# Post-LN block on 8 cores: draining six instead of four queued layer-norm pieces per output slab

## The chip, the cores and the metric

The kernel runs on all 8 cores of one Trainium2 chip. Each core computes one of 8 batch rows with the same program; nothing is exchanged between cores. The time is the device time of the slowest core, in microseconds.

## The reference

One layer of a recurrent block with post-layer-norm, input x of shape (8, 2048, 1024). Cut to what matters:

```python
xg = gelu(x)
# for fwd and bwd: x1 = xg@Wx+bx; gates = sigmoid(x1@Wg..+b..); h = linear_scan(a, xin); y = h@Wo+bo
x2 = (x_fwd + x_bwd) / 2 + x
attn = gelu(x2) @ ld_W + ld_b + x
x = layernorm(x + attn)                        # LN1
y = clip((x @ sign(weights).T) * scale + bias, -100, 100)
x = layernorm(x + y)                           # LN2
```

## The kernel before

Everything is kept transposed: 1024 features in 8 slabs (index `o`, or `k` when contracted) of 128 partitions, 2048 tokens along the free axis, cut into two halves `h` of 1024 tokens. The stages follow one another: gelu of x, the two input projections, gates and scans forward and backward, the output projections, then the linear layer `Wld` with the first layer norm, then the sign-weight layer with the second.

`Builder` writes one instruction list per engine, in the order in which the Python code calls `bd.op` and `bd.mm_group`. An engine executes its list strictly in that order; semaphores make it wait for what other engines produce. There is no scheduler: where a call stands in the code is where the instruction stands in its engine's list.

The change lies in the linear stage (lines 799 to 878). For each half h and each output slab o:

- TensorE runs one group of 16 matmuls of 128x512 (line 152 emits every matmul), into PSUM buffer `slot = o % 2`; called group 0 to group 7 here. Group o needs that the VectorE operation at L838 of slab o-2 has read the buffer.
- In the second half only, the queue `bg` has pieces in it: `drain_bg(n)` takes up to n of them and emits their instructions at this place, ahead of the slab's own ScalarE and VectorE operations.
- ScalarE doubles the input slab (L833), VectorE adds PSUM, bias and that (L838) and so writes `r1`; this is what frees the PSUM buffer. ScalarE squares `r1` (L845 in the first half, L860 in the second).
- In the second half the statistics of two slabs (8 matmuls by a column of ones, into PSUM slots 2 and 3) follow each of groups 4, 5, 6 and 7, if `len(bg) <= 8`.

`bg` holds the first half's layer norm, 18 pieces in this order: 0 and 1 ScalarE on the sums (L605, L609), 2 VectorE variance (L612), 3 ScalarE Ln (L615), 4 ScalarE Exp (L619), 5 the split of the reciprocal deviation into a high and a low bf16 row (ScalarE L629, then VectorE L632), 6 its broadcast to 128 partitions (TensorE, 2 matmuls of the high and 2 of the low row, then the ScalarE copy L652), 7 VectorE product (L667), 8 the split of the product (L629, L632), 9 its broadcast (4 matmuls, L652), and 10 to 17 the four pairs of VectorE operations of 128x2048 that apply the norm: multiply (L704) and add (L711). The result is read first by the sign-weight stage, after all 8 groups.

Of the kernel before, what the change touches and what calls it, by code (L numbers as in the profile page):

```python
# [171 lines left out]
def build_program():  # L172
# [68 lines left out]
    def ps_ap(slot, lo, hi):  # L241
        return ps_t[slot].ap()[:, ps_off[slot] + lo: ps_off[slot] + hi]

    def vcol(nm, o):
        return vecs_sb[:, VCOL[nm] + o: VCOL[nm] + o + 1]
# [91 lines left out]
    def wtile(arena_ap, o, k):  # L337
        return arena_ap[:, o * 1024 + k * 128: o * 1024 + (k + 1) * 128]
# [154 lines left out]
    def sgn_prep(oc):  # L493
        if wtB[0] is None:
            wtB[0] = Buf("wt0", deps=woslabs[4:6])
            wtB[1] = Buf("wt1", deps=woslabs[6:8])
        sl = oc % 2
        bd.op("sync",
              lambda e, oc=oc, sl=sl:
              e.dma_start(wt_ap[sl], w_hbm["Wffn"].ap()[:, oc * 1024:(oc + 1) * 1024]),  # L500
              writes=[wtB[sl]], inc="dX", step=16)
        bd.op("vector",
              lambda e, oc=oc, sl=sl:
              e.tensor_scalar(A4.ap()[:, 8192 + oc * 1024: 8192 + (oc + 1) * 1024],
                              wt_ap[sl], 0.0, 0.5, ALU.is_ge, ALU.subtract),
              reads=[wtB[sl]], writes=[sgnB], inc="dv")
# [8 lines left out]
    def xc_dma(xcb, o, h, sl):  # L515
        bd.op("sync",
              lambda e, o=o, h=h, sl=sl:
              e.dma_start(xc56_ap[sl], x_hbm.ap()[o * 128:(o + 1) * 128,
                                                  h * HF:(h + 1) * HF]),
              writes=[xcb[sl]], inc="dX", step=16)  # L520
# [69 lines left out]
    def stats_tiles(src_ap_fn, src_buf, k, slot):  # L590
        tiles, treads = [], []
        for t in range(2):
            tiles.append((ones_sb.ap()[:],
                          src_ap_fn(k, t),
                          ps_ap(slot, t * 512, (t + 1) * 512)[0:1, :],
                          k == 0, k == CH - 1))
            treads.append([src_buf, onesB])
        bd.mm_group(tiles, treads, group_reads=(), writes=[PS[slot]])
# [182 lines left out]
    def drain_bg(n):  # L781
        for _ in range(n):
            if bg:
                bg.pop(0)()
# [11 lines left out]
    def emit_sq6_until(j):  # L796
        while sq6_emitted[0] <= j and sq6_pend:
            sq6_pend.pop(0)()
            sq6_emitted[0] += 1

    r1B_h, r1view_h = {}, {}
    for h in range(2):
# [8 lines left out]
        for o in range(CH):  # L811
            if o + 3 < CH:
                xc_dma(xc6, o + 3, h, (o + 3) % 4)
            sl = o % 2
            slot = o % 2
            tiles, treads = [], []
            for k in range(CH):
                for t in range(2):
                    tiles.append((wtile(A4.ap()[:, 0:8192], o, k),
                                  A3.ap()[:, k * 2048 + h * HF + t * 512:  # L820
                                          k * 2048 + h * HF + (t + 1) * 512],
                                  ps_ap(slot, t * 512, (t + 1) * 512),
                                  k == 0, k == CH - 1))
                    treads.append([g2[k * 2 + h], WldS[o]])
            bd.mm_group(tiles, treads, group_reads=(), writes=[PS[slot]])
            if h == 0 and len(pending_stats) > 1:
                pending_stats.pop(0)()
            if h == 0 and sgn_q:
                sgn_prep(sgn_q.pop(0))
            drain_bg(4)  # L830
            xsl = o % 4
            bd.op("scalar",
                  lambda e, sl=sl, xsl=xsl: e.activation(u_ap[sl], xc56_ap[xsl],  # L833
                                                         AF.Copy, scale=2.0),
                  reads=[xc6[xsl]], writes=[uB[sl]], inc="sc")
            bd.op("vector",
                  lambda e, slot=slot, sl=sl, o=o, r1view=r1view:
                  e.scalar_tensor_tensor(r1view[:, o * 1024:(o + 1) * 1024],  # L838
                                         ps_ap(slot, 0, 1024), vcol("ldb", o),
                                         u_ap[sl], ALU.add, ALU.add),  # L840
                  reads=[PS[slot], uB[sl], vecsB], writes=[r1B[o]], inc="dv")
            if h == 0:
                bd.op("scalar",
                      lambda e, o=o, sl=sl, r1view=r1view:
                      e.activation(rsq_ap[sl], r1view[:, o * 1024:(o + 1) * 1024],  # L845
                                   AF.Square),
                      reads=[r1B[o]], writes=[rsqB[sl]], inc="sc")

                def _stats(o=o, sl=sl, r1view=r1view, r1B=r1B):
                    stats_tiles(lambda k, t, r1view=r1view:  # L850
                                r1view[:, k * 1024 + t * 512: k * 1024 + (t + 1) * 512],
                                r1B[o], o, 2)
                    stats_tiles(lambda k, t, sl=sl: rsq_ap[sl][:, t * 512:(t + 1) * 512],
                                rsqB[sl], o, 3)
                pending_stats.append(_stats)
            else:
                sq6_pend.append(lambda o=o, r1view=r1view, r1B=r1B: bd.op(
                    "scalar",
                    lambda e, o=o, r1view=r1view:
                    e.activation(rsq6_ap[o], r1view[:, o * 1024:(o + 1) * 1024],  # L860
                                 AF.Square),
                    reads=[r1B[o]], writes=[rsqS6[o]], inc="sc"))
                if o >= 2:
                    emit_sq6_until(o - 2)

                def _stats(o=o, r1view=r1view, r1B=r1B):
                    emit_sq6_until(o)
                    stats_tiles(lambda k, t, r1view=r1view:
                                r1view[:, k * 1024 + t * 512: k * 1024 + (t + 1) * 512],
                                r1B[o], o, 2)  # L870
                    stats_tiles(lambda k, t: rsq6_ap[k][:, t * 512:(t + 1) * 512],
                                rsqS6[o], o, 3)
                pending_stats.append(_stats)
                if o >= 4 and len(bg) <= 8:
                    while len(pending_stats) > (CH - 1 - o):
                        pending_stats.pop(0)()
# [201 lines left out]
```

How the kernel before makes its waits and increments, by code:

```python
        def thunk(e, wl=tuple(wl), emits=tuple(emits), tok=tok, step=step):  # L118
            for s, v in wl:
                e.wait_ge(sems[s], v)
            inst = None
            for em in emits:
                inst = em(e)
            if tok is not None:
                inst.then_inc(sems[tok[0]], step)
# [18 lines left out]
        def thunk(e, head=tuple(head), per=tuple(per), tiles=tuple(tiles),  # L144
                  tok=tok):
            for s, v in head:
                e.wait_ge(sems[s], v)
            inst = None
            for (lh, rh, oa, st, sp), wl in zip(tiles, per):
                for s, v in wl:
                    e.wait_ge(sems[s], v)
                inst = e.matmul(oa, lh, rh, start=st, stop=sp)
            inst.then_inc(sems[tok[0]], 1)
# [830 lines left out]
    def final_wait(e):  # L984
        for base in ("dO", "dX", "dG"):
            for j in range(Builder.DMA_POOL):
                nm = f"{base}{j}"
                if bd.counts.get(nm, 0):
                    e.wait_ge(bd.sems[nm], bd.counts[nm])
```

## Time and profile before

| what | us |
|---|---|
| median of 2 runs | 746.49 (746.29 to 746.69) |
| the profiled execution's own time | 744.0 |
| span of its slowest core (core 5) | 742.5 |
| spans of all cores | 722.7 to 742.5 |
| TensorE busy in the span | 629.4 |
| VectorE busy | 327.4 |
| ScalarE busy | 349.4 |

The time is the slowest core's; the span runs from that core's first to its last instruction. The shares of busy time are averages over stages that have different limits.

### The profile page before, as it was taken

Reading aid. Unit: us, or ns where it says so; the run is one execution under the profiler, and the core shown is the slowest. Engines: PE = TensorE matmul, PEld = TensorE weight load, DVE = VectorE, ACT = ScalarE, POOL = GpSimd, SP = SyncE. Lnnn points to the kernel's source line nnn. Section 1 sums busy time; section 2 is a strip of 40 time slices with the busy share of each in tenths; the row PEclk is TensorE's granted clock in tenths of the full one; section 3 lists DMA queues with packets and bytes.
Section 4 is the critical chain, followed back from the end, with each engine's and each line's share of the span. In section 5 each row is a group of like instructions: output and inputs, shape, how many; then the busy total and the mean of one; then the engine's idle time right before and its main releaser. Section 6 shows DMA issues by size and latency. Waiting matters only on the chain.

```text
span 742.5 us, 7192 instructions; the slowest of 8 cores (722.7 to 742.5 us)
## 1 busy us (share of the span) xinstructions
PE 629.4 (85%) x2720; PEld 265.2 (36%) x2720; DVE 327.4 (44%) x191; ACT 349.4 (47%) x258; POOL 50.8 (7%) x96
## 2 busy tenths in 40 slices
PE   0349999999999999999999858997998769679660
PEld 0004444444444444444444323443332224224220
DVE  0000000003767767767763120213348638838846
ACT  2442322326687687787771120203375347747710
POOL 2010000000000000000131110100000000000000
PEclk9999999999999999999999998999999888869855
DMA  8997000003222322322439999815753000003205
GB/s 175 249 199 116 1 0 1 1 0 43 43 31 42 43 30 42 43 31 40 72 47 168 203 200 150 178 45 173 212 166 104 1 0 1 1 0 113 115 0 226
DMA packets 23217, 61.33 MB, mean 83 GB/s; under 512 B 2704, under 2 KB 2704, under 8 KB 23184
## 3 DMA queue, kind: packets, MB, share of 16 engines
q0 software_dynamic: 13248, 25.17, 22.9%
q1 hardware_dynamic: 8208, 29.42, 13.2%
q10 hardware_dynamic: 1728, 6.29, 2.8%
q8 instruction: 22, 0.36, 0.2%
q14 instruction: 11, 0.09, 0.0%
HBM read 75.55 MB, written 8.39 MB: 113 GB/s over the span
## 4 chain that ended last, share of the span: by engine, by line
PE 63%; DMA 15%; DVE 11%; issue 5%; ACT 4%; SPq 0%; DVEq 0%; ACTq 0%; POOLq 0%
PE psA L152 32%; PE psB L152 31%; DMA A<-x 6%; DMA A<-Wof 4%; DMA A<-Wob 3%; DVE A L944 2%; DMA A<-Wffn 2%; DVE A L743 2%; DVE A L704 1%; DVE A L757 1%; DVE A L838 1%; ACT srbf L629 1%; DVE srbf L632 1%; DVE A L950 1%; DVE srows L612 1%
## 5 line engine op out<-in xcount | busy, mean ns | idle before, releaser
L152 PE MATMUL psA<-A 128*128 128x512 bf16 x1536 | 359.3, 392 | 60.9 <-ACT A L329 21.5
L152 PEld LDWEIGHTS psA<-A 128*128 128x128 bf16 x1536 | 150.4, 100 | 263.9 <-issue 97.6
L152 PE MATMUL psB<-A 128*128 128x512 bf16 x1024 | 227.8, 381 | 2.0 <-DVE A L568 2.0
L152 PEld LDWEIGHTS psB<-A 128*128 128x128 bf16 x1024 | 100.6, 98 | 124.5 <-issue 5.3
L429 DVE TENSOR_SCALAR A<-A,dvec_sb 128x2048 f32<-128x2048 f32 x16 | 20.6, 1286 | 170.4 <-ACT A L425 170.4
L440 DVE TENSOR_TENSOR A<-A 128x2048 f32<-128x2048 f32 x16 | 36.7, 2292 | 51.0 <-ACT A L433 51.0
L573 ACT ACTIVATE A<-A,dvec_sb 128x1024 bf16<-128x1024 f32 x16 | 18.4, 1148 | 83.1 <-DVE A L568 83.1
L152 PE MATMUL psB<-A,ones_sb 128*1 128x512 bf16 x128 | 37.7, 439 | 13.7 <-DVE A L950 11.2
L425 ACT ACTIVATE A<-psB,vecs_sb 128x2048 f32<-128x2048 f32 x16 | 31.5, 1967 | 32.0 <-PE psB L152 32.0
L431 ACT ACTIVATE A<-A 128x2048 f32<-128x2048 f32 x16 | 30.6, 1910 | 23.8 <-DVE A L429 23.8
L568 DVE SCALAR_TENSOR_TENSOR A<-psA,A 128x1024 f32<-128x1024 f32 x8 | 9.8, 1225 | 72.1 <-PE psA L152 59.1
L438 DVE TENSOR_TENSOR A<-A 128x2048 f32<-128x2048 f32 x16 | 36.6, 2284 | 0.0
L452 DVE TENSOR_TENSOR_SCAN A<-A 128x2048 bf16<-128x2048 f32 x8 | 35.4, 4425 | 0.9 <-DVE A L440 0.2
L446 DVE TENSOR_TENSOR_SCAN A<-A 128x2048 bf16<-128x2048 f32 x8 | 35.4, 4426 | 0.8
L356 ACT ACTIVATE A<-psB,vecs_sb 128x2048 bf16<-128x2048 f32 x8 | 15.7, 1967 | 40.9 <-PE psB L152 40.9
L356 ACT ACTIVATE A<-psA,vecs_sb 128x2048 bf16<-128x2048 f32 x8 | 15.7, 1967 | 35.8 <-PE psA L152 35.8
L421 ACT ACTIVATE A<-psA,vecs_sb 128x2048 f32<-128x2048 f32 x16 | 31.5, 1970 | 0.2
L433 ACT ACTIVATE A<-A 128x2048 f32<-128x2048 f32 x16 | 30.6, 1910 | 0.2
L838 DVE SCALAR_TENSOR_TENSOR A<-psA,vecs_sb,A 128x1024 bf16<-128x1024 f32 x16 | 20.5, 1281 | 20.5 <-ACT A L833 9.6
L329 ACT ACTIVATE A<-A 128x1024 bf16<-128x1024 f32 x16 | 16.0, 1048 | 24.5 <-DMA A<-x 24.5
L152 PEld LDWEIGHTS psB<-A,ones_sb 128*1 128x1 bf16 x128 | 10.3, 91 | 39.9 <-issue 32.5
L933 ACT ACTIVATE A<-psA,dvec_sb 128x1024 f32<-128x1024 f32 x16 | 19.2, 1202 | 10.2 <-PE psA L152 6.4
(59 smaller groups left out, 353.4 us busy)
## 6 DMA issues: line engine op xcount, KB each, us to landing
A<-x SPq DMA_DIRECT2D x40, 512.0 KB, 8.2
A<-x ACTq DMA_DIRECT2D x8, 512.0 KB, 15.2
A<-Wof POOLq DMA_DIRECT2D x16, 256.0 KB, 11.2
A<-Wob POOLq DMA_DIRECT2D x16, 256.0 KB, 13.2
A<-Wffn SPq DMA_DIRECT2D x8, 512.0 KB, 6.1
out<-A SPq DMA_DIRECT2D x8, 512.0 KB, 3.8
A<-Wxf POOLq DMA_DIRECT2D x8, 256.0 KB, 32.4
A<-Wxb POOLq DMA_DIRECT2D x8, 256.0 KB, 22.5
```

What stands on the lines that cost most here:

```text
L152: inst = e.matmul(oa, lh, rh, start=st, stop=sp)
L356: e.activation(xb_arena.ap()[:, o * 2048:(o + 1) * 2048], pst.ap()[:], AF.Identity, bias=vcol(bias_name, o)),
L421: e.activation(gx_ap[p], psA.ap()[:], AF.Sigmoid, bias=vcol(bgx_name, o)),
L425: e.activation(ga_ap[p], psB.ap()[:], AF.Sigmoid, bias=vcol(bga_name, o)),
L429: e.tensor_single_scalar(ab_ap[p], ga_ap[p], ae_col(d, o), ALU.mult),
L431: bd.op("scalar", lambda e, p=p: e.activation(tb_ap[p], ab_ap[p], AF.Square), reads=[abB[p]], writes=[tbB[p]], inc="sc")
L433: bd.op("scalar", lambda e, p=p: e.activation(tb_ap[p], tb_ap[p], AF.Sqrt, bias=1.0, scale=-1.0), reads=[tbB[p]], writes=[tbB[p]], inc="sc")
L438: e.tensor_mul(gx_ap[p], gx_ap[p], xb_arena.ap()[:, o * 2048:(o + 1) * 2048]),
L440: bd.op("vector", lambda e, p=p: e.tensor_mul(gx_ap[p], gx_ap[p], tb_ap[p]), reads=[gxB[p], tbB[p]], writes=[gxB[p]], inc="dv")
L446: e.tensor_tensor_scan(hview, ab_ap[p], gx_ap[p], 0.0, ALU.mult, ALU.add),
L452: e.tensor_tensor_scan(hview[:, ::-1], ab_ap[p][:, ::-1], gx_ap[p][:, ::-1], 0.0, ALU.mult, ALU.add),
L838: e.scalar_tensor_tensor(r1view[:, o * 1024:(o + 1) * 1024], ps_ap(slot, 0, 1024), vcol("ldb", o), u_ap[sl], ALU.add, ALU.add),
```

## The change

One number, in the loop over output slabs of the linear stage. In the first half `bg` is empty and the call does nothing.

```diff
@@ -827,7 +827,7 @@
                 pending_stats.pop(0)()
             if h == 0 and sgn_q:
                 sgn_prep(sgn_q.pop(0))
-            drain_bg(4)
+            drain_bg(6)
             xsl = o % 4
             bd.op("scalar",
                   lambda e, sl=sl, xsl=xsl: e.activation(u_ap[sl], xc56_ap[xsl],
```

The pieces then stand so in the code:

| slab | before | after |
|---|---|---|
| 0 | 0 to 3 | 0 to 5 |
| 1 | 4 to 7 | 6 to 11 |
| 2 | 8 to 11 | 12 to 17 |
| 3 | 12 to 15 | none |
| 4 | 16, 17 | none |

## Rows read from the trace of the kernel before

**Rows 1.** The page of the slowest core: span, and the chain that ended last.

```profile
span 742.5 us, 7192 instructions; the slowest of 8 cores (722.7 to 742.5 us)
...
PE 63%; DMA 15%; DVE 11%; issue 5%; ACT 4%; SPq 0%; DVEq 0%; ACTq 0%; POOLq 0%
```

**Rows 2.** The chain of waits, linear stage, second half: start, us, engine, tile, line.

```profile
578.63 1.29 DVE A L838
580.06 6.48 PE psA L152 x16
586.54 1.82 PE psB L152 x8
588.36 3.56 PE psA L152 x16
...
593.74 3.57 PE psA L152 x16
```

**Rows 3.** Timeline of TensorE, core 5: start, duration, instruction, idle before and releaser.

```profile
549.94 7.08 PE L152 MATMUL psA<-A 128*128 128x512 bf16 x32
...
558.51 0.59 PE L152 MATMUL psB<-srbf,onesb_sb 1*128 1x512 bf16 x2 [0.73 <-DVE srbf L632]
559.03 3.63 PE L152 MATMUL psA<-A 128*128 128x512 bf16 x16
...
569.67 3.61 PE L152 MATMUL psA<-A 128*128 128x512 bf16 x16 [1.72 <-DVE A L838]
...
580.06 6.48 PE L152 MATMUL psA<-A 128*128 128x512 bf16 x16 [4.96 <-DVE A L838]
```

**Rows 4.** Timeline of VectorE, core 5, the same stretch.

```profile
557.15 1.21 DVE L632 TENSOR_TENSOR srbf<-srows,srbf 1x1024 bf16<-1x1024 f32 x1 [0.81 <-ACT srbf L629]
558.29 1.21 DVE L667 TENSOR_TENSOR srows<-srows 1x1024 f32<-1x1024 f32 x1
561.26 1.28 DVE L838 SCALAR_TENSOR_TENSOR A<-psA,vecs_sb,A 128x1024 bf16<-128x1024 f32 x1 [1.76 <-ACT A L833]
562.46 1.20 DVE L632 TENSOR_TENSOR srbf<-srows,srbf 1x1024 bf16<-1x1024 f32 x1
563.60 2.27 DVE L704 TENSOR_TENSOR A<-A 128x2048 bf16<-128x2048 bf16 x1
566.04 2.29 DVE L711 TENSOR_TENSOR A<-A 128x2048 bf16<-128x2048 bf16 x1 [0.17 <-DVE A L704]
568.25 1.28 DVE L838 SCALAR_TENSOR_TENSOR A<-psA,vecs_sb,A 128x1024 bf16<-128x1024 f32 x1
569.44 2.28 DVE L704 TENSOR_TENSOR A<-A 128x2048 bf16<-128x2048 bf16 x1
571.83 2.29 DVE L711 TENSOR_TENSOR A<-A 128x2048 bf16<-128x2048 bf16 x1
...
582.21 2.29 DVE L711 TENSOR_TENSOR A<-A 128x2048 bf16<-128x2048 bf16 x1
```

**Rows 5.** Timeline of ScalarE, core 5, the layer norm's short chain.

```profile
552.86 1.15 ACT L615 ACTIVATE srows<-srows 1x1024 f32<-1x1024 f32 x1
553.91 1.04 ACT L833 ACTIVATE A<-A 128x1024 f32<-128x1024 f32 x1
554.86 1.04 ACT L619 ACTIVATE srows<-srows 1x1024 f32<-1x1024 f32 x1
555.99 1.06 ACT L629 ACTIVATE srbf<-srows 1x1024 bf16<-1x1024 f32 x1
559.19 1.02 ACT L652 ACTIVATE A<-psB 128x1024 f32<-128x1024 f32 x1 [2.14 <-PE psB L152]
```

**Rows 6.** Stretches, core 5: length, busy per engine, granted clock, DMA share, GB/s.

```profile
575.00:580.00 5.00, 0.10 (x1) 0.00 (x0) 4.89 (x4) 0.00 (x0) 0.00 (x0) 0.91 0.00 0
580.00:587.00 7.00, 6.94 (x19) 2.46 (x20) 5.88 (x4) 3.15 (x4) 0.00 (x0) 0.58 0.01 2
```

**Rows 7.** Timeline of TensorE on core 6: its group 5.

```profile
582.22 4.89 PE L152 MATMUL psA<-A 128*128 128x512 bf16 x16 [4.95 <-DVE A L838]
```

## The prediction

> **What bounds the kernel now.** I read the page first: the chain that ended last is 63% TensorE and only 11% VectorE [rows 1]. Over the whole span TensorE sets the pace, but the change touches one short stretch, so its own limit has to be found there. The chain of waits gives it: from 578.63 it runs L838 on VectorE, then group 5, its statistics, group 6, its statistics, group 7, each right behind the other [rows 2]. So from 580.06 on TensorE alone sets the end of the stage, and ahead of it an L838 does. TensorE's timeline says what that cost: 1.72 us idle ahead of group 4 and 4.96 us ahead of group 5, both times waiting for L838 [rows 3]. VectorE's timeline says why L838 was late: it is a 1.28 us instruction, but its list has the apply pieces in front of it, two 128x2048 operations of 2.28 and 2.29 us to each pair [rows 4]. The two PSUM buffers let TensorE run two groups ahead of L838, and no further. The stretches show the last cost: the granted clock was 0.91 in the mostly idle 575 to 580 and 0.58 in 580 to 587, so group 5 took 6.48 us where group 6 took 3.56 [rows 2, 6].
>
> **The change, part by part.** It adds and removes no instruction. It moves pieces 4 and 5 from slab 1 to slab 0, 8 to 11 from slab 2 to slab 1, and 12 to 17 from slabs 3 and 4 to slab 2. No piece issues a DMA, so the queues are not passed. The statistics stay behind groups 4 to 7: at slab 4 `bg` is empty with 4 as with 6. I follow VectorE's new list, with the spacings (start to start) of the old one.
>
> *Slab 0.* Exp now stands straight behind Ln, ahead of L833. Ln ends at 552.86 + 1.15 = 554.01; the step from Exp's end to L629 was 0.09 [rows 5], so Exp runs 554.10 to 555.14, L629 555.23 to 556.29. L632 began 0.10 after L629's end [rows 4, 5]: now 556.39, 0.76 earlier than before. L838 of slab 0 follows 1.14 later (the spacing L632 to L667), at 557.53; its other input, L833, is done about 557.2, so nothing waits. This end is worth a gain of 0.76, and none of it lasts, as slab 1 shows.
>
> *Slab 1.* L667 follows 1.20 later (the spacing L838 to L632), at 558.73, and ends 559.94. The second split is now here, bare: L629 560.04 to 561.08, L632 at 561.18, L704 1.14 later at 562.32, L711 2.39 later (spacing of 569.44 and 571.83) at 564.71, L838 of slab 1 2.21 later (566.04 to 568.25) at 566.92 [rows 4]. It ends 568.20; before, it began at 561.26. The copy L652 that L711 needs starts 0.68 after its matmuls start (558.51 and 559.19) [rows 3, 5], so at 562.53 + 0.68 = 563.21, and ends 564.23: it is hidden by L704 with 0.48 to spare.
> On TensorE both broadcasts stand between groups 1 and 2. Groups 0 and 1 end at 557.02 as before [rows 3]. Group 2, which before ran between the two broadcasts and hid the second split, waits for its low row: 562.53 + 0.52 = 563.05 instead of 559.03. This wait is new, 4.0 us, and behind it stand groups 2 and 3. At 3.56 us group 2 ends 566.61, ahead of what group 3 waits for (568.20, and 0.14 more as from 569.53 to 569.67 [rows 3, 4]). Group 3 starts at 568.34 and ends 571.90. Should this sparse stretch lower the clock, group 2 at half pace takes 7.12 us and ends 570.17, group 3 by 577.3 at the latest; the next step hides that too. So I cost the new wait at 0; bare, without the cover of slab 2, it would cost the 4.0.
>
> *Slab 2.* Three pairs now stand ahead of its L838: from 566.92 + 1.19 = 568.11, 3 x (2.39 + 2.21) = 13.80, so L838 starts at 581.91 and ends 583.19. Group 4 needs its buffer: it starts at 583.33 instead of 569.67, 13.66 later, and TensorE has been idle since 571.90, 11.43 us. Nothing else in its list can fill this; the statistics stand behind group 4.
>
> *Slabs 3 to 7.* Nothing is in front of L838 any more. The waits ahead of groups 5, 6 and 7 go, and next late is TensorE itself. Group 4 has to take the slow clock that group 5 had. A gap of 11.4 us in the trace's second half of this stage isn't there; nearest is the 4.96 us one, whose restart took 6.48 us on core 5 and, after 4.95, 4.89 on core 6 [rows 3, 7]. The lower bound is a group at full clock, 3.56; the upper bound is half clock through the group and its 8 statistics, 2 x (3.56 + 1.82) = 10.76 instead of 6.48 + 1.82 = 8.30. I take 6.48, the same core's own row. Then group 5 starts 583.33 + 8.30 = 591.63, group 6 5.38 later at 597.01, group 7 at 602.39, against 593.74 [rows 2].
>
> *The sum.* The point from which TensorE runs unheld moves from 580.06 to 583.33, +3.27, and one group with statistics more stands behind it, +5.38: together +8.65. The apply pieces end earlier (VectorE starts its last at 579.70 instead of 582.21 [rows 4]), but their first reader is the stage after group 7, which gives nothing back. Everything behind group 7 is the same work in the same order, waiting for group 7. So 742.5 + 8.65 = 751.15 span, 744.0 + 8.65 = 752.65 for the profiled execution. The median of the runs was 746.49, 2.49 above that execution; on the median's level the forecast is 755.1 us, 1.2% longer.
>
> The clock, weighed. Group 5 came after 4.96 us idle, and the granted clock of its stretch was 0.58, a mix of the levels 1.2 and 2.4 GHz; on core 6 the restart after the same idle cost less than half as much, 4.89 - 3.56 = 1.33 us [rows 3, 6, 7]. So a restart nearly at full clock can't be ruled out by rows, and I leave it a chance (D below). The Trainium skill (TensorE: Matmul & The Clock Gate, "HAM oscillation — how this bites in real kernels") says that a long enough wait puts the engine back to the low level and that every restart after one is charged. By that rule alone D would have no chance and the sum would stay 755.1; the traces bear it out on both cores, in unequal size.
>
> **The rivals.**
>
> *A, the rotation of buffers hides it: 746.5.* Two PSUM buffers let one L838 run late while the next group computes, and total VectorE work is unchanged. For it: 1.72 us ahead of group 4 was little although a pair stood in front. Against: the buffer covers about one group (3.56 us), and three pairs are 13.8. It would need a place of slack behind group 7 of 8.65 us, and the chain shows none [rows 2]. The Trainium skill (Perfetto Trace Analysis, "Optimizing Tensor Performance", Matmuls) advises rotating groups through different PSUM banks so that evacuation overlaps the next group; taken alone it gives this rival, 746.5, and the idle 4.96 ahead of group 5 already disagrees.
>
> *B, faster: the wait at group 5 goes and isn't replaced.* Place: group 5. Price: 4.96 idle and 6.48 - 3.56 = 2.92 of slow clock, 7.88, so 738.6. That is the whole price if group 4 starts as early as before; it decides from the point where group 4's own shift and slow restart stay under 7.88. My figure for those is 13.66 + 2.92 = 16.58. For it: L838 of slab 3 has nothing ahead of it now. Against: it stands behind L838 of slab 2, and that behind three pairs.
>
> *C, the clock lasts longer.* Half clock through group 4 and its statistics: +2.46, 757.6. For it: a gap over twice as long. Against: rows 6 and 7, where the full clock was back by the group's end or before it. An extreme of it, half clock through groups 5, 6 and 7 as well, adds 3 x 5.38 = 16.1: 773.7.
>
> *D, group 4 at full clock.* 6.48 - 3.56 = 2.92 less: 752.2. Core 6's 4.89 lies halfway to it.
>
> **How the numbers follow.** Forecast 0.74, A 0.08, B 0.03, C 0.09 (0.02 of it the extreme), D 0.06. The range runs from D less half of the 2.7 us that executions of the kernel differ by (744.0 to 746.69), 750.9, to C plus the same, 759.0; outside are A, B and the extreme, 0.13, and a few hundredths for a mistake in the list. 2% is about what a measurement of this kernel can tell from no change: 731.6 and 761.4. No case is below the first, 0.01; only the extreme of C and errors of my list are above the second, 0.04; within, 0.95.
>
> **What would show it.** In the profile of the changed kernel: both broadcasts between groups 1 and 2, with about 5 us from group 1's end to group 2's start of which TensorE works little; L838 of slab 2 some 15 us after L838 of slab 1 with six L704/L711 between; TensorE idle about 11 us ahead of group 4 and released by L838; a granted clock near 0.6 just behind; no idle ahead of groups 5 to 7; from group 0's start to group 7's 52.5 us instead of 43.8. Wrong if group 4 starts less than 30 us after group 0, if group 5 still waits, or if the distance from group 7 to the end changes by over 2 us.

## The result, and the profile after

The changed kernel took 752.07 us (median of 11 runs) against 745.58 before (10 runs): 1.0089 times as long, 95% interval 1.0066 to 1.0113. The forecast was 755.1, or +8.65 us; by the ratio the change costs 6.6 us (0.0089 x 745.58), by the ends of the interval 4.9 to 8.4. So it is slower, clear of the noise and within 2%. (In some executions some or all of the cores run at a lowered clock; these are left out of every ratio here, and the one profile that fell on one, that of e2, isn't read.)

The page of the changed kernel looks like the one of before: the chain that ended last has the same shares by engine. Nothing in it points to the place.

```profile
span 748.4 us, 7140 instructions; the slowest of 8 cores (729.4 to 748.4 us)
...
PE 63%; DMA 15%; DVE 11%; issue 5%; ACT 4%; SPq 0%; DVEq 0%; ACTq 0%; POOLq 0%
```

The chain of waits does (core 2, the slowest; columns as in [rows 2]):

```profile
568.27 1.28 DVE A L838
569.55 2.21 DVE A L704
571.85 2.29 DVE A L711
574.14 2.21 DVE A L704
576.45 2.29 DVE A L711
578.74 2.21 DVE A L704
...
583.25 1.29 DVE A L838
584.68 5.80 PE psA L152 x16
590.48 1.82 PE psB L152 x8
...
597.67 3.56 PE psA L152 x16
```

Before, one L838 led straight to group 5 [rows 2]. Now the chain runs from one L838 through the whole row of apply operations to the next, and this one releases group 4. TensorE's timeline, same core (a matmul record is missing from groups 0 and 1; group 0 starts at 551.2):

```profile
551.44 6.85 PE L152 MATMUL psA<-A 128*128 128x512 bf16 x31 [0.16 <-issue]
...
559.04 0.59 PE L152 MATMUL psB<-srbf,onesb_sb 1*128 1x512 bf16 x2 [0.21 <-DVE srbf L632]
562.51 1.01 PE L152 MATMUL psB<-srbf,onesb_sb 1*128 1x512 bf16 x2 [2.89 <-ACT srbf L629]
563.83 1.01 PE L152 MATMUL psB<-srbf,onesb_sb 1*128 1x512 bf16 x2 [0.31 <-DVE srbf L632]
564.77 8.98 PE L152 MATMUL psA<-A 128*128 128x512 bf16 x31
584.68 5.80 PE L152 MATMUL psA<-A 128*128 128x512 bf16 x16 [10.92 <-DVE A L838]
```

Where [rows 3] had 1.72 us idle ahead of group 4 and 4.96 ahead of group 5, there is one wait of 10.92 ahead of group 4 and none after it. Groups 2 and 3 took 8.98 instead of 7.1: behind the sparse stretch between the broadcasts they started slow. VectorE's timeline has its two marks in place:

```profile
562.47 1.21 DVE L632 TENSOR_TENSOR srbf<-srows,srbf 1x1024 bf16<-1x1024 f32 x1 [1.25 <-ACT srbf L629]
563.61 2.27 DVE L704 TENSOR_TENSOR A<-A 128x2048 bf16<-128x2048 bf16 x1
...
568.27 1.28 DVE L838 SCALAR_TENSOR_TENSOR A<-psA,vecs_sb,A 128x1024 bf16<-128x1024 f32 x1
```

And the stretches (columns as in [rows 6]) show TensorE empty while VectorE works, then a restart that is partly on the lower clock (0.65 granted in the mean), then the full one:

```profile
574.00:584.00 10.00, 0.00 (x0) 0.00 (x0) 9.79 (x6) 0.00 (x0) 0.00 (x0) 0.75 0.01 4
584.70:591.00 6.30, 6.30 (x19) 2.25 (x20) 1.37 (x2) 3.88 (x4) 0.00 (x0) 0.65 0.01 3
591.00:603.00 12.00, 11.95 (x55) 4.49 (x54) 3.51 (x3) 4.22 (x5) 0.00 (x0) 1.00 0.00 0
```

Against the forecast, both counted from group 0's start:

| event | forecast | measured, core 2 |
|---|---|---|
| low row of the second broadcast starts | 12.6 | 12.6 |
| L838 of slab 1 starts | 17.0 | 17.1 |
| L838 of slab 2 starts | 32.0 | 32.1 |
| group 4 starts | 33.4 | 33.5 |
| group 4 takes | 6.48 | 5.80 |
| group 7 starts | 52.5 | 51.8 |
| from group 7's start to the end | 148.8 | 145.4 |

I read two lengths from TensorE's timeline of every core: the stage (group 0's start to group 7's start) and the tail (from there to the core's end). Means of the eight cores:

| kernel | stage, us (range) | tail, us (range) | sum |
|---|---|---|---|
| before | 43.16 (42.6 to 43.7) | 148.19 (147.2 to 148.9) | 191.35 |
| changed | 51.89 (50.9 to 52.4) | 146.55 (145.4 to 148.7) | 198.44 |

The stage grew by 8.7 us, as forecast; the tail, with the same instructions in the same order, was 1.6 shorter. The sum is +7.1. On the slowest core of each profile the forecast was +8.65 and the span grew by 5.9: +8.0 in the stage, -3.4 in the tail, and +1.3 ahead of group 0 (549.94 to 551.2), which the change doesn't touch.

### The profile page after: what moved, and what is told of

Same layout as the page of the kernel before. It is cut to its first block, busy times and chain, and to the rows that moved or that the text cites. A ratio compares the mean times of both kernels' runs of the same rounds, so it can differ in the third digit from the quotient of the medians.

```text
span 748.4 us, 7140 instructions; the slowest of 8 cores (729.4 to 748.4 us)
## 1 busy us (share of the span) xinstructions
PE 624.3 (83%) x2667; PEld 264.9 (35%) x2720; DVE 327.3 (44%) x191; ACT 349.7 (47%) x258; POOL 50.8 (7%) x96
## 4 chain that ended last, share of the span: by engine, by line
PE 63%; DMA 15%; DVE 11%; issue 5%; ACT 4%; SPq 0%; DVEq 0%; ACTq 0%; POOLq 0%
PE psA L152 33%; PE psB L152 31%; DMA A<-x 6%; DMA A<-Wof 4%; DMA A<-Wob 3%; DVE A L944 2%; DMA A<-Wffn 2%; DVE A L704 2%; DVE A L757 2%; DVE A L743 1%; DVE A L838 1%; DVE srbf L632 1%; DMA out<-A 1%; ACT srbf L629 1%; DVE srows L612 1%
## 5 line engine op out<-in xcount | busy, mean ns | idle before, releaser
L152 PE MATMUL psB<-A,ones_sb 128*1 128x512 bf16 x128 | 35.5, 420 | 13.5 <-DVE A L950 11.7
L452 DVE TENSOR_TENSOR_SCAN A<-A 128x2048 bf16<-128x2048 f32 x8 | 35.4, 4425 | 0.9 <-DVE A L440 0.2
L446 DVE TENSOR_TENSOR_SCAN A<-A 128x2048 bf16<-128x2048 f32 x8 | 35.4, 4425 | 0.8
L838 DVE SCALAR_TENSOR_TENSOR A<-psA,vecs_sb,A 128x1024 bf16<-128x1024 f32 x16 | 20.4, 1280 | 23.7 <-PE psA L152 19.5
L833 ACT ACTIVATE A<-A 128x1024 f32<-128x1024 f32 x16 | 16.6, 1044 | 17.4 <-DVE A L838 17.4
```

Of the source, the lines that this page charges most:

```text
L152: inst = e.matmul(oa, lh, rh, start=st, stop=sp)
L446: e.tensor_tensor_scan(hview, ab_ap[p], gx_ap[p], 0.0, ALU.mult, ALU.add),
L452: e.tensor_tensor_scan(hview[:, ::-1], ab_ap[p][:, ::-1], gx_ap[p][:, ::-1], 0.0, ALU.mult, ALU.add),
L838: e.scalar_tensor_tensor(r1view[:, o * 1024:(o + 1) * 1024], ps_ap(slot, 0, 1024), vcol("ldb", o), u_ap[sl], ALU.add, ALU.add),
```

## The experiments

The theory: TensorE may run two groups ahead of L838, L838 stands in VectorE's list behind the apply pieces, so the pieces drained ahead of one L838 set when the next group but one can start. The rivals: the broadcast wait costs by itself (rival 1); the stage's VectorE work is the bound whatever its order (rival 2). Each ratio is to the kernel before, run beside it on the same chip. Edits are to the line `drain_bg(4)` unless another is shown. The stage and tail are as above.

**e1: the burst spread out.**

```diff
-            drain_bg(4)
+            drain_bg((6, 6, 2, 2, 2, 0, 0, 0)[o])
```

> Slabs 0 and 1 drain 6 pieces as in the changed kernel, slabs 2 to 4 one apply pair each instead of three at once. Measure: group 0's start to group 7's start, 42.6 to 43.7 us before, 50.9 to 52.4 changed. Theory 1 (the burst of six apply operations ahead of slab 2's L838 is the whole cost, the bare wait between the broadcasts costs nothing): groups 4, 5, 6 released one after the other some 5.8 us apart, distance about 41, total 2 to 3 us under before. Rival 1 (the bare wait of 4 us between groups 1 and 2 is a cost of its own): distance 45 or more, total not under before.

Stage 41.15 (41.0 to 41.2), ratio 0.9956 (0.9924 to 0.9987). On core 2 the groups come 5.8 us apart, each released by an L838 with one pair in front of it:

```profile
569.98 3.61 PE L152 MATMUL psA<-A 128*128 128x512 bf16 x16 [1.11 <-DVE A L838]
575.77 3.61 PE L152 MATMUL psA<-A 128*128 128x512 bf16 x15 [0.36 <-DVE A L838]
581.56 3.61 PE L152 MATMUL psA<-A 128*128 128x512 bf16 x16 [0.36 <-DVE A L838]
```

The rows are groups 4, 5 and 6 (the middle one has a matmul record missing). The first two slabs are those of the changed kernel, with its broadcast wait. The stage is 10.7 us shorter than in the changed kernel and 2 shorter than before. What changed is only how six operations are cut up between three L838s: the burst is the cost.

**e2 and e7: one pair per slab.**

```diff
-            drain_bg(4)
+            drain_bg((4, 4, 2, 2, 2, 2, 2, 0)[o])
```

> Drains 4, 4, 2, 2, 2, 2, 2: the broadcasts where they were, then one apply pair in front of each L838 of slabs 3 to 6. Theory 1: each L838 then ends before TensorE is through with the group in between, no group waits, distance from group 0 to group 7 about 34.5, total about 9 us under before (ratio 0.988). Rival 1 predicts nothing other here. Rival 2 (the stage's VectorE work as a whole is the bound, so its order moves nothing): distance 43, total as before.

> The version with one pair per slab (drains 4, 4, 2, 2, 2, 2, 2) once more, since its first profile was of a disturbed execution. Theory 1: no group waits over 1 us, distance 34 to 36 us, total 0.99 times before, the fastest of all here.

Ratios 0.9914 (0.9876 to 0.9952) and 0.9927 (0.9901 to 0.9954). e7's stage was 37.6 (37.1 to 38.0): no group waited over 1 us, but it is 3 longer than I expected. I had followed the groups and left out that the statistics of slab 5 stand ahead of group 7 and need its L838; they waited 1.22 us. And VectorE's row of pairs started late (its timeline in e7, core 0, L838 of slab 2):

```profile
559.39 1.28 DVE L838 SCALAR_TENSOR_TENSOR A<-psA,vecs_sb,A 128x1024 bf16<-128x1024 f32 x1 [3.81 <-ACT A L833]
```

It waits for a ScalarE doubling that stands in ScalarE's list behind the copy L652 of the second broadcast. e9 takes this up.

**e3: only the early pieces early.**

```diff
-            drain_bg(4)
+            drain_bg((6, 4, 2, 4, 2, 0, 0, 0)[o])
```

> Drains 6, 4, 2, 4, 2: pieces 4, 5, 8 and 9 early as in the changed kernel, both broadcasts between groups 1 and 2, but all apply pairs where they stood before. Theory 1: the bare wait of about 4 us appears between groups 1 and 2 and is taken up by the later wait ahead of group 5: distance 43 to 44.5, total 0 to +1. Rival 1: distance 47, total +4.

Stage 46.14 (45.5 to 46.8), ratio 1.0043 (1.0018 to 1.0068). A miss for both: the early broadcasts alone cost 3.0 us, neither nothing nor 4. In the changed kernel L838 of slab 1 has a pair in front of it; here it has none, and still starts only 15.8 us after group 0, against 11.3 before. ScalarE's timeline and VectorE's, core 3:

```profile
544.78 1.02 ACT L652 ACTIVATE A<-psB 128x1024 f32<-128x1024 f32 x1 [2.56 <-PE psB L152]
545.70 1.99 ACT L833 ACTIVATE A<-A 128x1024 f32<-128x1024 f32 x2
```

```profile
546.85 1.28 DVE L838 SCALAR_TENSOR_TENSOR A<-psA,vecs_sb,A 128x1024 bf16<-128x1024 f32 x1 [3.32 <-ACT A L833]
```

The list of ScalarE hands TensorE's wait on to VectorE: L652 waits for the broadcast, L833 for its turn behind L652, L838 for L833; everything on VectorE then is about 3 us late, group 5 too.

**e10: the same, with L833 out of that queue.** Two causes were open, and this run parts them.

```diff
-            drain_bg(4)
             xsl = o % 4
...
                   reads=[xc6[xsl]], writes=[uB[sl]], inc="sc")
+            drain_bg((6, 4, 2, 4, 2, 0, 0, 0)[o])
```

> As e3 (pieces 4, 5, 8, 9 early, pairs where they were before), with L833 ahead of the pieces. Two causes are open for e3's 3.0 us. Cause a: L838 of slab 1 waits for an L833 that stands in ScalarE's list behind the copy of the second broadcast: then the distance falls from 46.1 to 43.5 to 44.5. Cause b: TensorE's wait between the broadcasts, by group 2's late end: then it stays at 46.

Stage 45.29 (44.4 to 45.7), ratio 1.0001 (0.998 to 1.0022): between the two figures. L838 of slab 1 starts 13.3 us after group 0 instead of 15.8 and no longer waits, but the one of slab 2 now waits for group 2, and TensorE's rows, core 3, say why that one is late:

```profile
566.46 1.28 DVE L838 SCALAR_TENSOR_TENSOR A<-psA,vecs_sb,A 128x1024 bf16<-128x1024 f32 x1 [0.38 <-PE psA L152]
```

```profile
561.31 11.88 PE L152 MATMUL psA<-A 128*128 128x512 bf16 x48
573.12 1.89 PE L152 MATMUL psB<-A,ones_sb 128*1 128x512 bf16 x8
578.63 6.53 PE L152 MATMUL psA<-A 128*128 128x512 bf16 x16 [3.62 <-DVE A L838]
```

Groups 2 to 4 took 11.8 us against 10.7 at full clock here, and on the other seven cores the slow start of group 2 cost 1.5 to 2.7 instead of 1.1. So both causes are there, one behind the other: taking the first away gives back 0.85 of the 3.0 us, and then the late and slow group 2 holds the same chain. The 0.85 is a lower figure for the first cause, since the edit has a price of its own: L833 now stands ahead of the layer norm's short chain too, and group 2 starts 14.5 us after group 0 where it was 13.56 in e3.

**e4: the burst one slab later.**

```diff
-            drain_bg(4)
+            if o != 2:
+                drain_bg(6)
...
                   reads=[PS[slot], uB[sl], vecsB], writes=[r1B[o]], inc="dv")
+            if o == 2:
+                drain_bg(6)
```

> The changed kernel with slab 2's six apply operations emitted behind slab 2's L838 instead of ahead of it. Theory 1: group 4 no longer waits for them, group 5 does, and is released near where group 4 was; one pair of group and statistics fewer stands behind the wait, so the distance is 5.4 us shorter than the changed kernel's, 46 to 47, total 3.3 over before less whatever the stretch behind group 7 gives back. Rival 2: distance as in the changed kernel, 52. For the stretch from group 7's start to the end (147.2 to 148.9 before, 145.4 to 148.7 changed, same instructions): if it depends only on how the clock falls in it, every run here scatters between 145 and 149; if the changed kernel's order itself shortens it, e3 and e4 stand near 146.5 and e2 near 148.

Stage 48.67 (48.3 to 49.3), ratio 1.0098 (1.0066 to 1.013). TensorE, core 3:

```profile
576.02 6.42 PE L152 MATMUL psA<-A 128*128 128x512 bf16 x16 [7.87 <-DVE A L839]
```

The wait moved from group 4 to group 5, as it must if the burst sits behind the L838 that frees group 4's buffer (L839 is L838; the edit shifts the lines by one). The stage is 3.2 us shorter than the changed kernel's, not 5.4: the burst can't start before L838 of slab 2, and that one waits for group 2, late and slow as in e10. In the changed kernel the burst covers this; here it doesn't. In the whole time the gain doesn't show: e4's ratio can't be told from those of the changed kernel (1.0089 above, 1.0124 in e6).

**e5: only the burst.**

```diff
-            drain_bg(4)
+            drain_bg((4, 4, 10, 0, 0, 0, 0, 0)[o])
```

> Drains 4, 4, 10: both broadcasts stay where they were before the change, all four apply pairs stand ahead of slab 2's L838. Theory 1 (what holds group 4 is the row of apply operations in front of slab 2's L838; the early broadcasts add nothing to it, though alone they cost 3 us): four pairs from the old start of the first, so group 4 starts 33 to 34 us after group 0 as in the changed kernel, and the distance from group 0 to group 7 is 51 to 53. Rival 1 (the cost of the early broadcasts, 3.0 us in e3, adds up with the burst's): distance 49. The stretch behind group 7: if its length depends on how much TensorE does between its slow restart and the stage's end, it is as in the changed kernel, mean of the cores near 146.6; if chance alone made those short, it is near 148.2 as before.

Stage 51.77 (50.9 to 53.1), ratio 1.0127 (1.0089 to 1.0166). TensorE, core 5:

```profile
562.80 3.63 PE L152 MATMUL psA<-A 128*128 128x512 bf16 x16
581.93 6.25 PE L152 MATMUL psA<-A 128*128 128x512 bf16 x16 [15.51 <-DVE A L838]
```

With the broadcasts where they were before the change, the stage is as long as in the changed kernel (51.9). Early broadcasts cost 3.0 by themselves and nothing beside the burst. The tail was 148.37 (146.8 to 149.1), near the figure that I gave for chance and not near the 146.6; more on it below.

**e6: the changed kernel again.**

> The changed kernel once more, for its time on this chip and a second set of eight cores. Distance from group 0 to group 7 50.9 to 52.4. Stretch behind group 7: mean of the cores 146.2 to 147.0 if it belongs to the kernel, near 148.2 if the first profile's was chance. Total 1.009 times before.

Stage 51.78 (51.2 to 52.2), as in the first profile. The ratio is 1.0124 (1.0095 to 1.0152), a little above the 1.009 that I expected, and the tail 147.26 (146.3 to 149.5) lies between my two figures.

**e8 and e12: three and five pieces.**

```diff
-            drain_bg(4)
+            drain_bg(3)
```

> drain_bg(3). The pieces stand in slabs 0 to 5; the pair operations as 2, 3 and 3 in slabs 3, 4 and 5. Theory 1: groups 4 and 5 unheld, group 6 waits about 1.7 us and group 7 about 2.8, neither long enough for a slow restart; distance about 40.5, total 2 to 3 under before. Rival (fewer pieces per slab only spread the same waits): distance 43.

> drain_bg(5): both broadcasts between groups 1 and 2, then five apply operations ahead of L838 of slab 2 and three ahead of slab 3's. Theory 1: L838 of slab 1 starts 15.4 us after group 0 (behind its L833, as in e3), group 4 starts about 29.5 us after group 0, slow, group 5 straight behind; distance 48 to 49, total 5 over before, between 4 and 6 pieces. Rival 2 (order moves nothing): 43.

Three: stage 39.87 (39.5 to 40.1), ratio 0.9958 (0.9933 to 0.9983). Five: stage 48.81 (48.6 to 49.0), ratio 1.0068 (1.0045 to 1.0092). With before and changed the stage is 39.9, 43.2, 48.8, 51.9 us for 3, 4, 5, 6 pieces. The stages of both are where they were expected. What I had wrong in e8 is how they come about: group 6 waits 2.56 us, not 1.7, group 7 not at all (the statistics ahead of it do), and "neither long enough for a slow restart" failed: group 6 or 7 ran partly on the lower clock on all eight cores, 1.0 to 1.7 us longer than the 3.6 of such a row at full clock. TensorE, core 7:

```profile
576.35 5.30 PE L152 MATMUL psA<-A 128*128 128x512 bf16 x16 [2.56 <-DVE A L838]
```

In e12 group 5 isn't straight behind group 4 on every core: on five it waits 0.3 to 1.3 us, at full clock.

**e9 and e11: towards a faster kernel.** L833 ahead of the pieces, as in e10, with the pairs in slabs 3 to 6 (e9) or 2 to 5 (e11).

```diff
+            drain_bg((4, 4, 2, 2, 2, 2, 2, 0)[o])      # e9
+            drain_bg((4, 4, 4, 2, 2, 2, 0, 0)[o])      # e11
```

> As e7 (one pair each in slabs 3 to 6), and the ScalarE doubling L833 of a slab is emitted ahead of that slab's pieces. In e7, VectorE's L838 of slab 2 sat idle 3.81 us for an L833 that stood behind the second copy L652. Theory 1: that idle time goes, VectorE's row of pairs starts 3.8 us earlier, the statistics behind group 6 no longer wait, distance from group 0 to group 7 34 to 35 us (36 where group 2 falls on the slow clock), total 2 to 3 us under e7, ratio to before about 0.988. Rival (TensorE, not VectorE, sets e7's pace by now): distance 37 to 38 as in e7.

> L833 ahead of the pieces, pairs in slabs 2 to 5 instead of 3 to 6. Theory 1: L838 of slab 5 ends later than in e9, so the second statistics behind group 6 wait about 2 us: distance about 38, total 0.99 to 0.995 of before. If no wait but the number of pieces per slab counted, it would equal e9.

e9: stage 35.38 (34.6 to 36.0), ratio 0.9887 (0.9852 to 0.9922). e11: stage 40.19 (39.5 to 41.9), ratio 0.9943 (0.9918 to 0.9969); the stage is 2 us over the 38 that I expected. I had counted the wait of the statistics alone (1.22 us), but a pair now stands ahead of L838 of slab 2 as well, so group 4 waits 1.3 to 1.7 us, and groups 5 and 6 come 5.8 us apart instead of 5.4. TensorE in e11, core 2, group 4:

```profile
563.11 3.61 PE L152 MATMUL psA<-A 128*128 128x512 bf16 x16 [1.72 <-DVE A L838]
```

In e9 no group waits over 1 us; the slow start that is left is at group 2, on four of the cores (core 7):

```profile
552.93 5.31 PE L152 MATMUL psA<-A 128*128 128x512 bf16 x16
...
559.14 7.08 PE L152 MATMUL psA<-A 128*128 128x512 bf16 x32
```

Rival 2 (the stage's VectorE work is the bound whatever its order) falls with e1 and e9: the same operations make a stage of 35.4, 41.2 or 51.9 us. e9 has the shortest stage, and its time is 8.4 us (0.0113 x 741.93) under the kernel before, from the same instructions in another order. Its whole time can't be told from that of e2 or e7, whose intervals overlap with its own.

## Why the prediction was right, and what was off

**The place and the gate: right.** The step "three pairs now stand ahead of its L838" gave group 4 at 33.4 us after group 0; 33.5 was measured. e1 and e5 show from both sides that these operations are what holds it.

**The new wait costed at 0: right for this change, wrong beside it.** It was hidden by slab 2's burst, as said (e5). But "bare, without the cover of slab 2, it would cost the 4.0" failed: bare it cost 3.0 (e3), and it took two roads, the queue of ScalarE and the slow clock of group 2 (e10, e4). I had followed it on TensorE alone, and said of the sparse stretch only that it might lower the clock; it did, and groups 2 and 3 took 9.0 us.

**One more group behind the gate, +5.38: right in the table,** with group 4's restart 5.80 on the slowest core, 0.7 under the 6.48 that I took, and on the mean of the cores as forecast: the stage grew 8.7 us for 8.65. A slow restart is paid on both sides, at group 5 before and at group 4 after, so the sum hangs little on its size.

**The term that was off: the tail, costed at 0.** "Everything behind group 7 is the same work in the same order": true, but its time isn't fixed. In the first profile it was 1.6 us shorter on the mean of the cores, in e6 0.9 shorter. The prediction called a change of over 2 us here a sign of being wrong; the means stay under that, the two slowest cores don't (148.8 and 145.4). Stage and tail of e6 add up to 199.04, 7.7 over before. So the forecast was above the first ratio's interval (to 8.4 us) by 0.2, and inside e6's (0.0095 to 0.0152 of 740.05, 7.0 to 11.2 us).

The remark that 2% is about what a measurement here can tell from no change was too cautious: with 10 and 11 runs the interval is 0.5% wide in all.

**The rivals.** A (the rotation of buffers hides it) fell: the second buffer covered group 3 and no more, and 10.9 us of idle time stood behind it. The Trainium skill's advice to rotate banks (Perfetto Trace Analysis, "Optimizing Tensor Performance", Matmuls) was followed before and after; the runs add that the evacuation must also come on time in its own engine's list. B fell: the wait ahead of group 5 did go, and its replacement was larger. C fell: group 4 took 5.80 us and not the 7.12 of half clock, its statistics the usual 1.82, and the stretch behind them at 1.00 ends the extreme too. D fell: group 4 took 4.85 to 6.35 on the eight cores (from its start to the next instruction's), never 3.56. By the rule of the Trainium skill (TensorE: Matmul & The Clock Gate, "HAM oscillation — how this bites in real kernels") D had no chance, and the trace agrees.

## What to carry to other kernels

Where an engine runs its list in order, background work must be dealt out by time between two releases of the busiest engine, not by count of pieces: here one pair of 4.6 us per group and statistics of 5.4 is hidden (e9), and three pairs ahead of one release make the stage 10.7 us longer than the same three ahead of three (changed kernel and e1). The kernel before already paid for two pairs ahead of one release: its 4.96 us of idle time ahead of group 5. Before moving a piece earlier, look in every list at what stands behind it: a wait on TensorE reached VectorE through a copy in ScalarE's list. A sparse stretch isn't only its own length; here the groups behind it mostly started on the lower clock (groups 2 and 3 took 9.0 us instead of 7.1).

## What was unexpected: the tail moves though nothing in it changes

The same instructions behind group 7 took 145.2 to 150.5 us on the single cores of the 13 profiles read. The rows that differ most are the statistics and the last broadcast of the final layer norm. Before (core 5), then changed (core 2):

```profile
648.37 6.89 PE L152 MATMUL psB<-A,ones_sb 128*1 128x512 bf16 x18 [0.92 <-DVE A L950]
...
713.77 7.16 PE L152 MATMUL psB<-srows,onesf_sb 1*128 1x512 f32 x8 [3.92 <-ACT srows L619]
```

```profile
658.07 5.39 PE L152 MATMUL psB<-A,ones_sb 128*1 128x512 bf16 x18 [0.92 <-DVE A L950]
...
720.99 5.91 PE L152 MATMUL psB<-srows,onesf_sb 1*128 1x512 f32 x8 [3.92 <-ACT srows L619]
```

The granted clock of the two was 0.58 and 0.50 before, the lower level throughout in the last broadcast, and 0.74 and 0.61 in the changed kernel. I then sorted the cores by which group the last slow restart fell on, and by how long that group took to the next instruction's start. The 56 cores of seven profiles fall into place; the eight of an eighth, e12, whose slow restart is at group 4 too, don't:

| restart at | kernels | restarted group took | cores | mean tail (range) |
|---|---|---|---|---|
| group 5 | before, e3, e4, e10 | under 5.45 | 16 | 147.57 (147.1 to 148.3) |
| group 5 | the same | 5.7 to 6.5 | 16 | 148.65 (148.0 to 150.5) |
| group 4 | changed, e6, e5 | under 5.45 | 9 | 148.91 (148.6 to 149.5) |
| group 4 | the same | 5.5 to 6.5 | 15 | 146.49 (145.4 to 147.1) |
| group 4 | e12 | under 5.45 | 4 | 147.32 (146.8 to 147.7) |
| group 4 | e12 | 5.8 to 6.3 | 4 | 147.25 (146.4 to 149.2) |

With the restart one group earlier the order turns round, in the seven profiles. In e12 it doesn't: its short restarts have tails of 146.8 to 147.7, all below those of the third line, and a long one has 149.2. So the division, made after the runs, isn't a rule, and what sets the tail stays open. The two readings that I had put down beforehand fared no better. If the changed order itself shortened the tail, e3 and e4 should have stood near 146.5; they had 147.94 and 148.36. If the work between the slow restart and the stage's end set it, e5 should have had 146.6; it had 148.37. What the rows of the two cores above show is where most of the difference lies: 2.75 of their 3.4 us are in two short stretches that ran on the lower clock for longer or shorter. What it means for a forecast is plain: the mean of the eight cores moved between 146.6 and 148.8 over the 13 profiles, so about 1 us either way, and more on a single core, can come from stretches that the change doesn't touch.
